# A four-stage graph network on one core: the combined node pass stores 136-column rows whole, and the attention scalars from a compact buffer

## The chip, the core and the metric

One core of a Trainium2 chip runs the whole network in one launch. The metric is the device time of that launch in microseconds (us). Engines are named as in the profile: PE multiplies matrices, DVE, ACT and POOL work element by element, SP only issues transfers, and 16 DMA engines move the data. POOL also issues the gathers and scatters by index.

## What is computed

There are 50,000 nodes with 128 features and 25,000 edges, sorted by destination. Four graph layers follow each other, each added to its input and normalised over the features:

```python
x = _layernorm(x + L0(x, src, dst, edge_weight, ...))
x = _layernorm(x + L1(x, ...))            # five rounds of propagation
x = _layernorm(x + L2(x, edge_attr_128, src, dst, ...))
x = _layernorm(x + L3(x, edge_index, ...))

# L3, attention with 4 heads of 32 columns:
xt = (x @ W.T + bias).reshape(n, H, C)
alpha_src = jnp.sum(xt * a_src, axis=-1)
alpha_dst = jnp.sum(xt * a_dst, axis=-1)
alpha = leaky_relu(alpha_src[row] + alpha_dst[col], 0.2)
# softmax of alpha over the edges of one destination, then
out = segment_sum(xt[row] * alpha[..., None], col)
```

So L3 needs, for each node, 128 columns of xt and 4 scalars as a source (136 columns with the 4 scalars as a destination).

## The kernel before

The kernel is a sequence of stages, each a block in which every engine runs a program of its own and waits on semaphores. Edge stages go over 200 tiles of 125 edges. Node stages go over the 50,000 rows in 30 chunks (`chunk`, lines 682 to 686): partition p owns 390 consecutive rows, and a chunk is 13 of them per partition, so that a chunk's rows of one partition are consecutive in DRAM. The last 80 rows are a chunk of their own. Node buffers are cut out of the tile `big` by `areas`, three slots each.

The change is in the combined node pass (lines 1850 to 2143). It finishes L2 and begins L3 for each chunk c:

- SP (`load`, `store`): waits until x3 of chunk c is ready, stores it (L1904), issues the two loads for chunk c+3 (x2n, L1898, and agg, L1899), waits until the transformed rows of chunk c are ready, and stores them: `xt_d`, 132 columns (L1908), and `ad_d`, 4 columns (L1909). All five go through one queue. Both stores read the same buffer O3, whose rows are 136 columns wide, so neither reads consecutive memory: a partition's data are 13 pieces of 528 bytes, and 13 pieces of 16 bytes.
- POOL: scales for the normalisation of chunk c (`ln_scale`, L743, L744, L746, L749), then the sums of chunk c+2 (L1930, L1933, and after a wait for its two loads L1937, L1941).
- DVE: for chunk c+1 `rows` (L2001, statistics L1989, L2011), which wait for POOL and PE, then for chunk c `transformed`: bias added from PSUM into O3 (L2019), and a 1x1 memset (L2025) that only carries the signal `d_o` to SP.
- ACT: copies of transposes out of PSUM for chunk c+1 (L2036), between them the normalisation of chunk c (L2042), which waits for L749, then the copies L2053.
- PE: transposes and products of chunk c+1 (L2106, L2116), then of chunk c (L2127, L2137).

The next stage (lines 2146 to 2192) gathers, for each of the 200 tiles of edges, the 132-column rows of `xt_d` by source into G (L2162) and the 4 columns of `ad_d` by destination into AD (L2165), both issued by POOL in turn; ACT copies the rows into `xts` (L2192), DVE adds the scalars (L2180).

Of the kernel before, what the change touches and what calls it, by code (L numbers as in the profile page):

```python
# [7 lines left out]
P, D = 128, 128  # L8
N, E = 50000, 25000
TE = 125  # L10
T = E // TE
GR = 4
U = 2 * GR
# [9 lines left out]
HEADS, CH = 4, D // 4  # L23
# [3 lines left out]
NJ = 13  # L27
CHUNKS = NC_ // NJ
SLOTS = 3
# [6 lines left out]
def build(nc, x0, src, dst, ea, ew, w0, b0, w1, b1, gamma, beta, w2, b2, we, be, coef, linw, linb, asrc, adst, out):  # L36
# [3 lines left out]
    def sb(name, shape, dt=F32):  # L40
        return ctx.enter_context(nc.sbuf_tensor(name, shape, dt))
# [3 lines left out]
    def sem(name):  # L45

        phase.append(nc.alloc_semaphore(name=name))
        return phase[-1]
# [16 lines left out]
    def dram(name, shape, dt=F32):  # L65
        return nc.dram_tensor(name, shape, dt).ap()

    with ctx:
# [7 lines left out]
        x1 = dram("x1", (N, D))  # L76
        x2n = dram("x2n", (N, D + 1))
        x3 = dram("x3", (N, D))
        xt_d = dram("xt_d", (N, D + HEADS))
        ad_d = dram("ad_d", (N, HEADS))  # L80
        lastpos = dram("lastpos", (N, 1), I32)
        pair_d = dram("pair_d", (T * P, 2))
# [32 lines left out]
        G = sb("G", [P, RG, D + HEADS])  # L115
# [19 lines left out]
        col = sb("col", [P, 8])  # L135
# [546 lines left out]
        def chunk(t, c, w):  # L682

            if c is None:
                return t[TAIL0:N, 0:w].unsqueeze(1)
            return t[0:TAIL0, :].rearrange("(p n) f -> p n f", n=NC_)[:, bass.ds(c * NJ, NJ), 0:w]
# [15 lines left out]
        def areas(widths, at=0, slots=2):  # L702

            got = []
            for w in widths:
                got.append([big[:, at + s * NJ * w:at + (s + 1) * NJ * w].rearrange("p (n f) -> p n f", f=w)
                            for s in range(slots)])
                at += slots * NJ * w
            return got
# [311 lines left out]
        flatY, flatG = Y[:].rearrange("p s f -> p (s f)"), G[:].rearrange("p s f -> p (s f)")  # L1021
# [9 lines left out]
        at = TG * P + TG * T // 2  # L1031
# [617 lines left out]
        at = U * CW  # L1649
# [198 lines left out]


        DX = D + 2 * HEADS  # L1850
        X2L, YL, X3, O3 = areas([D + 1, D, D, DX], slots=SLOTS)
        at = SLOTS * NJ * (3 * D + 1 + DX)
        W2 = big[:, at:at + D]
        B2 = big[:, at + D:at + 2 * D]
        LW = big[:, at + 2 * D:at + 5 * D].rearrange("p (b i) -> p b i", b=3)
# [28 lines left out]
        with nc.Block() as block:  # L1884
            @block.sync
            def _(sp):
                with nc.allow_non_contiguous_dma(reason="short columns"):
                    sp.dma_start(W2, w2).then_inc(d_w, 16)
                    sp.dma_start(B2, b2.partition_broadcast(P)).then_inc(d_w, 16)
                    sp.dma_start(LW, linw.rearrange("b o i -> o b i")).then_inc(d_w, 16)  # L1890
                    sp.dma_start(CF, coef.partition_broadcast(P)).then_inc(d_w, 16)
                    sp.dma_start(AC[:, 0, :], asrc.rearrange("b q h c -> (q h c) b")).then_inc(d_w, 16)
                    sp.dma_start(AC[:, 1, :], adst.rearrange("b q h c -> (q h c) b")).then_inc(d_w, 16)
                    sp.dma_start(AC[:, 2, :], linb.rearrange("b o -> o b")).then_inc(d_w, 16)
                def load(c, s, n):
                    np_, nj = size(c)
                    sp.wait_ge(d_t, before_chunk(c, QA))
                    sp.dma_start(X2L[s][0:np_, 0:nj, :], chunk(x2n, c, D + 1)).then_inc(d_ld[s], 16)  # L1898
                    sp.dma_start(YL[s][0:np_, 0:nj, :], chunk(agg, c, D)).then_inc(d_ld[s], 16)  # L1899

                def store(c, s, n, later):
                    np_, nj = size(c)
                    sp.wait_ge(d_x3[s], n + 1)
                    sp.dma_start(chunk(x3, c, D), X3[s][0:np_, 0:nj, :]).then_inc(d_sx[s], 16)  # L1904
                    if later:
                        load(*later)
                    sp.wait_ge(d_o[s], n + 1)
                    sp.dma_start(chunk(xt_d, c, D + HEADS), O3[s][0:np_, 0:nj, 0:D + HEADS]).then_inc(d_so[s], 16)  # L1908
                    sp.dma_start(chunk(ad_d, c, HEADS), O3[s][0:np_, 0:nj, D + HEADS:DX]).then_inc(d_so[s], 16)  # L1909
                turns = CHUNKS // SLOTS  # L1910
                for u in range(SLOTS):
                    load(u, u, 0)
                with sp.Fori(0, turns - 1) as i:
                    for u in range(SLOTS):
                        store(SLOTS * i + u, u, i, (SLOTS * i + SLOTS + u, u, i + 1))
                for u in range(SLOTS):
                    store(CHUNKS - SLOTS + u, u, turns - 1, (None, 0, turns) if u == 0 else None)
                store(None, 0, turns, None)
                for s in range(SLOTS):
                    sp.wait_ge(d_sx[s], 16 * (turns + (1 if s == 0 else 0)))  # L1920
                    sp.wait_ge(d_so[s], 32 * (turns + (1 if s == 0 else 0)))
# [38 lines left out]
            def _(dve):  # L1960
# [53 lines left out]
                def transformed(c, s, n):  # L2014
                    np_, nj = size(c)
                    dve.wait_ge(d_so[s], 32 * n)
                    for q, js in groups(c, 3):
                        dve.wait_ge(d_q, before_chunk(c, QB) + q + 1)
                        ins = nc.vector.tensor_tensor(  # L2019
                            O3[s][0:np_, js[0]:js[-1] + 1, :],  # L2020
                            bank(6 + q % 2, 3 * DX).rearrange("p (j f) -> p j f", f=DX)[0:np_, 0:len(js), :],
                            B3X[0:np_, :].unsqueeze(1).to_broadcast([np_, len(js), DX]), ALU.add)
                        ins.then_inc(d_oc, 1)
                    dve.wait_ge(d_oc, before_chunk(c, QB) + len(groups(c, 3)))
                    nc.vector.memset(col[0:1, 7:8], 0.0).then_inc(d_o[s], 1)  # L2025
                one_ahead(dve, rows, transformed)

            @block.scalar
# [117 lines left out]
        XW = D + HEADS  # L2146
        xts = big[:, 0:T * XW].rearrange("p (t f) -> p t f", f=XW)
        AL = cf[:, 0:T * HEADS].rearrange("p (t h) -> p t h", h=HEADS)
        AD = sb("AD", [P, U, HEADS])
        e_idx, e_cp = sem("e_idx"), sem("e_cp")  # L2150
        e_got, e_gad = pool_sems("e_got", U), pool_sems("e_gad", U)
        with nc.Block() as block:
            @block.gpsimd
            def _(pool):
                with pool.Fori(0, IT) as i:
                    for j in range(U):
                        steady(pool, 2 * i + j // GR + 1)
                        if j % GR == 0:

                            pool.wait_ge(e_idx, 2 * i + j // GR + 1)  # L2160
                            pool.wait_ge(e_cp, 2 * i + j // GR + 1)
                        pool.indirect_dma_start(G[:, j, 0:XW], None, xt_d, bass.IndirectOffsetOnAxis(  # L2162
                            ap=ridx[:, j:j + 1], axis=0)).then_inc(e_got[j], 16)
                        steady(pool)
                        pool.indirect_dma_start(AD[:, j, :], None, ad_d, bass.IndirectOffsetOnAxis(  # L2165
                            ap=sidx[:, j:j + 1], axis=0)).then_inc(e_gad[j], 16)

            @block.vector
            def _(dve):
                nc.vector.tensor_copy(ridx[:], src_i[:, 0:U])  # L2170
                nc.vector.tensor_copy(sidx[:], dst_i[:, 0:U]).then_inc(e_idx, 2)
                credit(e_cp, 2)
                with dve.Fori(0, IT) as i:
                    for h in range(2):
                        js = slice(GR * h, GR * h + GR)
                        steady(dve, 16 * i + 16)
                        for q in range(GR * h, GR * h + GR):
                            dve.wait_ge(e_got[q], 16 * i + 16)
                            dve.wait_ge(e_gad[q], 16 * i + 16)
                        nc.vector.tensor_tensor(AL[:, bass.ds(U * i + GR * h, GR), :], G[:, js, D:XW], AD[:, js, :],  # L2180
                                                ALU.add)
                        nc.vector.tensor_copy(ridx[:, js], src_i[:, bass.ds(U * i + U + GR * h, GR)])
                        nc.vector.tensor_copy(sidx[:, js], dst_i[:, bass.ds(U * i + U + GR * h, GR)]).then_inc(e_idx, 1)

            @block.scalar
            def _(act):
                with act.Fori(0, IT) as i:
                    for h in range(2):
                        steady(act, 16 * i + 16)
                        for q in range(GR * h, GR * h + GR):  # L2190
                            act.wait_ge(e_got[q], 16 * i + 16)
                        nc.scalar.copy(xts[:, bass.ds(U * i + GR * h, GR), :], G[:, GR * h:GR * h + GR, :]).then_inc(e_cp, 1)  # L2192

# [231 lines left out]
```

## Time and profile before

| | |
|---|---|
| median of 3 timed runs | 9566.44 us (9566.18 to 9572.16) |
| the profiled execution's own time | 9559.96 us |
| its span in the trace | 9558.2 us |
| POOL busy | 6656.3 us, 70% |
| PE busy | 5802.3 us, 61% |
| DVE busy | 4949.1 us, 52% |
| combined node pass in the trace | about 7928 to 8500 us |
| gather stage of L3 | about 8500 to 9000 us |

How to read it: busy shares over the whole span mix stages with different limits. In a row of the timeline the columns are the start, the duration, the engine, the line and operation, the tiles, the count, and in brackets the idle time before it with what ended it. A row of SP shows how long SP was held by issuing a transfer, not the transfer itself.

### The profile page before, as it was taken

To read this page: it belongs to the slowest core of one execution; us is meant where nothing else is said; L and a number is where in the kernel's file an instruction comes from. 1 tells how busy PE (TensorE), PEld (TensorE's weight loads), DVE (VectorE), ACT (ScalarE), POOL (GpSimd) and SP (SyncE) were. 2 spreads that over 40 slices of the span, in tenths; PEclk is the share of its full clock that TensorE was granted. 3 is DMA by queue.
4 is the path that set the end of the run, shared out by engine and by line. 5 is a ranking of instruction groups with operands and counts; after the bars stand their busy time and mean duration, and the time that the engine had idled before them with its cause. 6 is when DMAs were issued, how large, how long until landed. Compare 5 with 4: busy or idle time off the path is not lost. (4 is left out here: it accounts for less than half of the span.)

```text
span 9558.2 us, 109668 instructions
## 1 busy us (share of the span) xinstructions
PE 5802.3 (61%) x24229; PEld 4310.9 (45%) x24229; DVE 4949.1 (52%) x12073; ACT 2449.6 (26%) x6228; POOL 6656.3 (70%) x6509
## 2 busy tenths in 40 slices
PE   4646557767775777765776756677651775630190
PEld 2436224555554555544555544555540665630170
DVE  5668765553335743345733346533357774520277
ACT  0115000222224222233222233222246113420006
POOL 4767663577777777777777777777766777767566
PEclk8765776775555855556855557755555887865555
DMA  3127101567755756655668656778656227961017
GB/s 145 43 94 257 25 2 31 115 116 101 101 100 103 135 105 100 102 100 111 126 105 99 102 99 125 116 100 100 101 106 228 64 68 156 193 107 28 20 31 327
DMA packets 564302, 1024.19 MB, mean 107 GB/s; under 512 B 192219, under 2 KB 275724, under 8 KB 563556
## 3 DMA queue, kind: packets, MB, share of 16 engines
q0 software_dynamic: 192032, 330.29, 31.3%
q1 hardware_dynamic: 354372, 588.76, 20.0%
q10 hardware_dynamic: 17664, 102.61, 2.6%
q14 instruction: 159, 1.30, 0.1%
q8 instruction: 75, 1.23, 0.1%
HBM read 561.87 MB, written 471.67 MB: 108 GB/s over the span
## 5 line engine op out<-in xcount | busy, mean ns | idle before, releaser
L1018 POOL DMA_INDIRECT G<-tab,gidx x4000 | 3952.7, 988 | 1622.0 <-issue 1407.3
L1365 PE MATMUL PS<-M,G 128*128 128x128 f32 x6400 | 2226.2, 472 | 1344.2 <-DMA G<-tab,gidx 949.2
L1365 PEld LDWEIGHTS PS<-M,G 128*128 128x128 f32 x6400 | 1539.3, 310 | 2052.8 <-DMA G<-tab,gidx 1463.8
L1313 ACT ACTIVATE M<-ident,wz 128x128 f32<-128x128 f32 x3200 | 1021.4, 390 | 2382.4 <-DVE UO L1421 1238.9
L1421 DVE TENSOR_TENSOR_SCAN UO<-keyrow,UT,PS 128x512 f32<-128x512 f32 (+1 forms) x400 | 512.0, 1280 | 1296.5 <-PE PS L1365 1296.5
L1421 DVE TENSOR_TENSOR_SCAN UT<-keyrow,UO,PS 128x512 f32<-128x512 f32 (+1 forms) x400 | 512.0, 1280 | 1193.1 <-PE PS L1365 1193.1
L758 ACT ACTIVATE big<-big,nb,rs 128x128 f32<-128x128 f32 x1173 | 461.3, 480 | 426.3 <-POOL nb L749 358.7
L1443 DVE TENSOR_TENSOR Y<-PS,big 128x512 f32<-128x512 f32 x800 | 536.3, 670 | 14.6 <-PE PS L1386 7.5
L1105 POOL DMA_INDIRECT Y<-pair_d,G x400 | 402.6, 1007 | 201.5 <-issue 130.6
L1390 PE MATMUL PS<-ident,UT 128*128 128x128 f32 x1600 | 419.2, 417 | 9.6 <-DVE UT L1421 9.6
L1390 PE MATMUL PS<-ident,UO 128*128 128x128 f32 x1600 | 420.6, 418 | 0.0
L1368 PE MATMUL PS<-ident,G 128*128 128x128 f32 x800 | 192.1, 310 | 348.8 <-DMA G<-tab,gidx 298.6
L1331 ACT ACTIVATE M<-PS,tcol,scol 128x512 f32<-128x512 f32 x200 | 155.4, 777 | 834.5 <-PE PS L1368 834.5
L1257 PE MATMUL PS<-big 128*128 128x400 f32 x800 | 321.2, 527 | 44.6 <-DVE G L1151 27.4
L1390 PEld LDWEIGHTS PS<-ident,UT 128*128 128x128 f32 x1600 | 340.3, 227 | 15.6 <-DVE UT L1421 15.6
L1390 PEld LDWEIGHTS PS<-ident,UO 128*128 128x128 f32 x1600 | 345.0, 228 | 0.0
L2269 PE MATMUL PS<-ident,cf 128*100 128x128 f32 x8 | 2.0, 424 | 526.5 <-DVE cf L2215 526.5
L450 POOL DMA_INDIRECT G<-in_x,ridx x200 | 206.7, 1033 | 157.4 <-DVE ridx L520 95.2
L2313 POOL DMA_INDIRECT agg<-Y,sidx x200 | 197.3, 987 | 153.7 <-DVE Y L2364 105.3
L902 POOL DMA_INDIRECT gidx<-lastpos,src_i x200 | 229.9, 1150 | 103.1 <-issue 68.4
L1368 PEld LDWEIGHTS PS<-ident,G 128*128 128x128 f32 x800 | 110.1, 149 | 411.4 <-DMA G<-tab,gidx 359.8
L1384 PE MATMUL PS<-cf 128*128 128x512 f32 x400 | 260.9, 741 | 8.3 <-DVE UT L1421 4.2
(500 smaller groups left out, 11257.3 us busy)
## 6 DMA issues: line engine op xcount, KB each, us to landing
tab<-Y SPq DMA_DIRECT2D x1050, 256.0 KB, 2.9
big<-agg SPq DMA_DIRECT2D x90, 832.0 KB, 11.4
G<-tab,gidx POOLq DMA_INDIRECT x4000, 4.0
WR<-w_d SPq DMA_DIRECT2D x200, 256.0 KB
big<-x SPq DMA_DIRECT2D x60, 832.0 KB, 4.9
xt_d<-big SPq DMA_DIRECT2D x30, 858.0 KB
x2n<-big ACTq DMA_DIRECT2D x30, 838.5 KB, 3.5
big<-x2n SPq DMA_DIRECT2D x30, 838.5 KB, 11.9
```

The lines of the kernel that those rows point to most:

```text
L758: ins = nc.scalar.activation(X[0:np_, j, 0:D], V[0:np_, j, :], ACT.Identity, scale=rs[0:np_, s, j:j + 1], bias=nb[0:np_, s, j:j + 1])
L902: pool.indirect_dma_start(gidx[:, t:t + 1], None, lastpos, bass.IndirectOffsetOnAxis(ap=src_i[:, t:t + 1], axis=0)).then_inc(g_got, 16)
L1018: pool.indirect_dma_start(G[:, t % RG, 0:D], None, tab_in(k), bass.IndirectOffsetOnAxis(ap=gidx[:, t:t + 1], axis=0)).then_inc(l_got[t % R ...
L1105: pool.indirect_dma_start(GS[:, t, :], None, pair_d, bass.IndirectOffsetOnAxis(ap=G2[:, t:t + 1], axis=0)).then_inc(o_got, 16)
L1257: ins = nc.tensor.matmul(bank2(n % 2)[:, j, :], OH[:, 2 * n + j, :], CT, start=True, stop=True)
L1313: ins = nc.scalar.activation(M[:, GR * h + j, :], ident[:], ACT.Copy, scale=wz[:, bass.ds((NB * i + q) * GR + j, 1)])
L1365: ins = nc.tensor.matmul(PS[:, FT_[h], j, :], G[:, s, 0:D], M[:, GR * h + j, :], start=True, stop=True)
L1368: ins = nc.tensor.transpose(PS[:, FT_[h], j, :], G[:, s, 0:D], ident[:])
L1384: nc.tensor.matmul(bank(BK_[h]), QR[:, q % NG, :], BD, start=True, stop=False)
L1390: ins = nc.tensor.transpose(PS[:, BK_[h], j, :], UR[h][:, j, :], ident[:])
L1421: nc.vector.tensor_tensor_scan(S[h], keyrow[:, bass.ds(tile * P, GR * P)], half if k == 0 else bank(FT_[h]), S[1 - h][:, GR * P - 1:GR * P ...
L1443: nc.vector.tensor_tensor(group_of(Y, q % NG), PS[:, BK_[h], :, :], zt_at((NB * i + q) * GR).rearrange("p (s f) -> p s f", f=D), ALU.add). ...
```

## The change

Rows of `xt_d` become 136 columns wide, and the store takes the whole buffer O3, whose pieces of one partition then join into one run of 7072 bytes. The destination's scalars are copied by DVE (in place of the memset that carried the signal) into a compact buffer AO of 4 columns, and stored from it: one run of 208 bytes per partition. The gather takes 136 columns per row, into a view GX of the same tile G, and its readers are pointed at GX. The diff:

```diff
-        xt_d = dram("xt_d", (N, D + HEADS))
+        xt_d = dram("xt_d", (N, D + 2 * HEADS))
...
-        X2L, YL, X3, O3 = areas([D + 1, D, D, DX], slots=SLOTS)
-        at = SLOTS * NJ * (3 * D + 1 + DX)
+        X2L, YL, X3, O3, AO = areas([D + 1, D, D, DX, HEADS], slots=SLOTS)
+        at = SLOTS * NJ * (3 * D + 1 + DX + HEADS)
...
-                    sp.dma_start(chunk(xt_d, c, D + HEADS), O3[s][0:np_, 0:nj, 0:D + HEADS]).then_inc(d_so[s], 16)
-                    sp.dma_start(chunk(ad_d, c, HEADS), O3[s][0:np_, 0:nj, D + HEADS:DX]).then_inc(d_so[s], 16)
+                    sp.dma_start(chunk(xt_d, c, DX), O3[s][0:np_, 0:nj, :]).then_inc(d_so[s], 16)
+                    sp.dma_start(chunk(ad_d, c, HEADS), AO[s][0:np_, 0:nj, :]).then_inc(d_so[s], 16)
...
-                    nc.vector.memset(col[0:1, 7:8], 0.0).then_inc(d_o[s], 1)
+                    nc.vector.tensor_copy(AO[s][0:np_, 0:nj, :], O3[s][0:np_, 0:nj, D + HEADS:DX]).then_inc(d_o[s], 1)
...
+        GX = flatG[:, 0:U * DX].rearrange("p (s f) -> p s f", f=DX)
...
-                        pool.indirect_dma_start(G[:, j, 0:XW], None, xt_d, bass.IndirectOffsetOnAxis(
+                        pool.indirect_dma_start(GX[:, j, :], None, xt_d, bass.IndirectOffsetOnAxis(
...
-                        nc.vector.tensor_tensor(AL[:, bass.ds(U * i + GR * h, GR), :], G[:, js, D:XW], AD[:, js, :],
+                        nc.vector.tensor_tensor(AL[:, bass.ds(U * i + GR * h, GR), :], GX[:, js, D:XW], AD[:, js, :],
...
-                        nc.scalar.copy(xts[:, bass.ds(U * i + GR * h, GR), :], G[:, GR * h:GR * h + GR, :]).then_inc(e_cp, 1)
+                        nc.scalar.copy(xts[:, bass.ds(U * i + GR * h, GR), :], GX[:, GR * h:GR * h + GR, 0:XW]).then_inc(e_cp, 1)
```

No instruction changes its place in any engine's program, and the number of instructions stays.

## Rows read from the trace of the kernel before

**Rows 1.** Busy time by stretch: us, each engine's busy us, clock, DMA share, GB/s.
```profile
8200.00:8300.00 100.00, 66.50 (x425) 59.04 (x425) 51.14 (x236) 45.51 (x112) 73.49 (x45) 0.86 1.02 180
```
**Rows 2.** Transfers in the stretch 8000 to 8400 us, packets by size, main queue.
```profile
DMA packets 85696, 76.70 MB, mean 192 GB/s; under 512 B 39958, under 2 KB 77247, under 8 KB 85695
...
q1 hardware_dynamic: 85695, 76.68, 102.9%
```
**Rows 3.** Timeline of SP's issues: start, us held, line, tiles.
```profile
7972.06 0.36 SPq L1904 DMA_DIRECT2D x<-big  x1
...
7973.23 1.06 SPq L1899 DMA_DIRECT2D big<-agg  x1
7979.74 0.41 SPq L1908 DMA_DIRECT2D xt_d<-big  x1
...
7986.45 0.34 SPq L1904 DMA_DIRECT2D x<-big  x1
...
8016.76 3.31 SPq L1904 DMA_DIRECT2D x<-big  x1
...
8430.70 2.14 SPq L1904 DMA_DIRECT2D x<-big  x1
...
8485.05 1.82 SPq L1909 DMA_DIRECT2D ad_d<-big  x1
8486.91 2.21 SPq L1904 DMA_DIRECT2D x<-big  x1
```
**Rows 4.** Timeline of POOL: start, us, line, idle before.
```profile
7965.27 0.21 POOL L749 TENSOR_TENSOR nb<-nb,rs 128x13 f32<-128x13 f32 x1
...
7979.64 0.22 POOL L749 TENSOR_TENSOR nb<-nb,rs 128x13 f32<-128x13 f32 x1
...
7993.65 0.22 POOL L749 TENSOR_TENSOR nb<-nb,rs 128x13 f32<-128x13 f32 x1
...
7999.40 3.40 POOL L1937 TENSOR_TENSOR big<-big 128x1664 f32<-128x1664 f32 x1 [2.25 <-DMA big<-agg]
...
8456.86 0.22 POOL L749 TENSOR_TENSOR nb<-nb,rs 128x13 f32<-128x13 f32 x1
```
**Rows 5.** Who waited for the load of agg (L1899): us, times.
```profile
  POOL big L1937: 100.3, 27
```
**Rows 6.** Transfers in the stretch 9400 to 9450 us (last node pass).
```profile
DMA packets 3586, 21.29 MB, mean 426 GB/s; under 512 B 388, under 2 KB 388, under 8 KB 3586
```
**Rows 7.** Transfers in 7980 to 7984 us, the first xt_d store.
```profile
DMA packets 1577, 0.83 MB, mean 208 GB/s; under 512 B 0, under 2 KB 1577, under 8 KB 1577
```
**Rows 8.** Issue of agg in 7971 to 7979 us: KB, us to landing.
```profile
big<-agg SPq DMA_DIRECT2D x1, 832.0 KB, 7.0
```
**Rows 9.** Timeline of ACT, the first copy of a turn.
```profile
7979.53 0.58 ACT L2036 COPY HT<-PS 128x512 f32<-128x512 f32 x1 [1.30 <-PE PS L2106]
...
7992.99 0.58 ACT L2036 COPY HT<-PS 128x512 f32<-128x512 f32 x1 [1.30 <-PE PS L2106]
```
**Rows 10.** Timeline of DVE around the signal d_o.
```profile
7992.97 0.06 DVE L2025 MEMSET col<- 1x1 f32 x1
7994.94 1.13 DVE L2001 SCALAR_TENSOR_TENSOR big<-PS,rin,big 128x128 f32<-128x128 f32 x4 [1.91 <-PE PS L2116]
```
**Rows 11.** Groups by line, a DVE copy of 132 elements.
```profile
L407 DVE COPY G<-carry 1x132 f32<-1x132 f32 x50 | 10.6, 212 | 0.8 <-PE PS L2381 0.8
```
**Rows 12.** Timeline of POOL in the last node pass, a short instruction twice.
```profile
9483.88 1.99 POOL L743 TENSOR_SCALAR rs<-mv 128x13 f32<-128x13 f32 x1 [0.61 <-DVE mv L735]
...
9489.62 0.26 POOL L743 TENSOR_SCALAR rs<-mv 128x13 f32<-128x13 f32 x1 [0.62 <-DVE mv L735]
```
**Rows 13.** Timeline of DVE in the last node pass, at the same moment.
```profile
9483.85 1.89 DVE L2399 TENSOR_TENSOR big<-big 128x1664 f32<-128x1664 f32 x1
```
**Rows 14.** Groups by line on POOL, the two gathers of the next stage.
```profile
L2162 POOL DMA_INDIRECT G<-xt_d,ridx x200 | 188.8, 944 | 87.4 <-issue 60.6 <-DVE note L170 26.8
L2165 POOL DMA_INDIRECT AD<-ad_d,sidx x200 | 188.8, 944 | 61.0 <-issue 51.5 <-ACT big L2192 9.5
```

## The prediction

> **What bounds the kernel now.** I read the busy times by stage first, since the change sits in one stage of some 570 us in a span of 9558.2 us. In the combined node pass no engine is near full: in 100 us PE is busy 66.50, DVE 51.14, ACT 45.51 and POOL 73.49, while the DMA engines stand at a share of 1.02 and move only 180 GB/s [rows 1]. The view of the transfers says why: of 85,696 packets in 400 us, 39,958 are under 512 bytes and another 37,289 under 2 KB, and the queue's packets took 102.9% of 16 engines' time [rows 2]. A full chunk stores 13 x 128 = 1664 pieces of 16 bytes and 1664 of 528 bytes; its x3 store and its two loads are only 128 long pieces each. The last node pass, whose transfers are all of that long kind, moves 426 GB/s [rows 6]. So the DMA engines are the bound here through the number of pieces, not through bytes.
>
> SP's timeline gives the pace. The x3 stores of chunks 3 and 26 start at 8016.76 and 8430.70 [rows 3]: 23 periods in 413.94 us, 18.0 us each. POOL's timeline shows where that reaches the engines: L1937 waits for the load of agg, 27 times and 100.3 us in all [rows 5], first at 7999.40 [rows 4].
>
> The same timeline also shows the pace without that wait, and this is what I use most. L749, which ends POOL's scaling of a chunk, starts at 7965.27, 7979.64 and 7993.65 [rows 4]. In these first periods the stores had not piled up yet, POOL ran nearly without a gap, and the period was 14.37 and then 14.01 us. The second one is POOL's own instructions end to end.
>
> **The change, part by part.**
>
> *Transfers of a chunk.* At 426 GB/s [rows 6] the three long transfers (832 + 838.5 + 832 KB, 2.56 MB) take 6.0 us. The first xt_d store went at 208 GB/s averaged over 7980 to 7984 [rows 7], but it was issued at 7979.74 [rows 3] and did not fill that stretch: 0.88 MB in some 3 to 4 us; I take 3. That leaves 18.0 - 6.0 - 3.0 = 9.0 us for the 1664 pieces of 16 bytes, so the smallest store is the dearest. After the change the xt_d store is 0.905 MB in 128 long pieces, 2.1 us, and ad_d is 128 pieces instead of 1664: 9.0 / 13 = 0.7 us if a piece keeps its price. Sum: 6.0 + 2.1 + 0.7 = 8.8 us a chunk, well under 14.01. The DMA engines stop being the bound.
>
> The Trainium skill (DMA: Bandwidth & Descriptors, Specifications) puts full rate at 512 bytes and more, with a read-modify-write below. By that rule the 528-byte store was at full rate already (2.1 us, and 9.9 for the small one) and making it whole wins nothing; the trace speaks against the rule for this store [rows 6, 7]. The sum would be the same by either, since both stores change together.
>
> *What is late next.* With the DMA free, POOL needs the load of chunk c+3 some 10.7 us after the x3 store of chunk c is issued: issue at 7986.45, and POOL was ready for L1937 at 7999.40 - 2.25 = 7997.15 [rows 3, 4]. In the one case with no strided store ahead, the x3 store went out at 7972.06 and agg was issued at 7973.23 [rows 3] and landed 7.0 us later [rows 8]: 8.2 us. So the load comes 2.5 us before it is needed, and POOL's wait (100.3 us) goes away. The other circle, ACT to PE to DVE and back, needs 7992.99 - 7979.53 = 13.46 us [rows 9], 0.55 less than POOL. POOL becomes the bound, at 14.01 us.
>
> From chunk 0 to chunk 28 L749 went from 7965.27 to 8456.86 [rows 4]: 491.59 us for 28 periods. After: 14.37 + 27 x 14.01 = 392.64 us. **Gain 98.95 us.** The last two chunks do not wait for loads, and I leave them.
>
> *The copy in place of the memset.* It moves 52 elements per partition. The nearest row is a copy of 132 elements in 212 ns [rows 11]; the memset took 60 ns [rows 10]. I take 0.2 us. On DVE itself it is covered: after the memset DVE idles 1.91 us for PE [rows 10]. But it may hold up POOL. In the last node pass a POOL instruction that began 0.03 us after a DVE addition of two SBUF tiles took 1.99 us, as long as that addition (1.89) [rows 12, 13], against 0.26 for the same instruction with no such neighbour [rows 12]. POOL is now the bound, so a copy that shuts it out costs its own time: 28 x 0.2 = 5.6 us. Bounds: 0, if it falls in a gap of POOL, and 5.9 (28 x 0.212). A gain is excluded, as the memset was already hidden. I take **5.6 us lost**, because POOL now has hardly a gap.
>
> [...]
>
> *The end of the pass.* The last x3 store's issue held SP 2.21 us, and the ad_d issue ahead of it 1.82 [rows 3]; free ones take 0.36 [rows 3] and about 0.4. That is 1.85 + 1.4 = 3.25 us; the two last copies take 0.3 back. **Gain 2.9 us.** Between nothing and 3.25.
>
> *The gather stage.* POOL issues a gather of 528-byte rows in 944 ns and one of 16-byte rows in 944 ns too [rows 14]: the length of a row does not matter to the issue, and the issues set the pace of that stage. 544 instead of 528 bytes: nothing. The ACT copy keeps its size and its cover; POOL waited for it 9.5 us in all [rows 14]. If a longer landing doubled that, 9.5 us would be lost: the bound on that side.
>
> *Sum.* -98.95 + 5.6 - 2.9 = -96.3 us. Against the profiled execution's 9559.96 this gives 9463.7; that execution lies 6.5 us below the median 9566.44, and timed runs are what is compared, so I carry the difference over: 9566.4 - 96.3 = **9470 us**, 1.0% faster. (About 0.2%, 19 us, is what a measurement of this kernel can tell from no change.)
>
> **The rivals.**
>
> *DVE waits for POOL at the copy, and the circle through DVE becomes the bound.* In the uncovered period the memset came at 7992.97, 0.7 us before POOL's L749 [rows 4, 10]. A copy there would wait for the POOL instruction under way, about 0.6 us, inside the 1.91 us of slack. If the phases slip so that it meets POOL's L1933 (3 us), L2001 starts about a microsecond late and the period grows to some 15.0 us. Gain 28 x (17.56 - 15.0) + 2.9 = 74.6: **9492 us**. For it: the lock seen in [rows 12, 13]. Against it: the 1.91 us.
>
> *The small store keeps its price* (its cost is not in the number of pieces, or its 13 pieces of a partition do not join, so that the change does not do what it says). Then a chunk needs 6.0 + 2.1 + 9.0 = 17.1 us of DMA instead of 18.0, the copy is hidden under POOL's waits, and some 25 periods win 0.9 us: 22 us, **9544 us**. Against it: the x3 store and the loads are of the same form, 13 rows side by side on both ends, and they do go as 128 pieces (8,448 packets over 2 KB in 22 chunks is 384 each) [rows 2].
>
> *Slower: a gather of longer rows costs POOL more to issue.* If a 544-byte row had to be cut in two and the issue of 944 ns doubled, the 200 gathers of L2162 would take 189 us more, and the sum would be +93: **9659 us**. It decides from 96.3 / 200 = 0.48 us per gather. Against it: 528-byte and 16-byte rows cost the same [rows 14], though one is 33 times as long.
>
> **How the numbers follow.** The forecast gets 0.76, the copy that waits 0.10, the small store that keeps its price 0.12, the dearer gather 0.02. Range: the fast end is the sum without the copy's cost and with the whole end gain, 9566 - 102 = 9464, less some 8 us for the spread between single executions and for a faster PE clock in the last chunks: 9456. The slow end takes in the first rival and loads that come a microsecond late in 14 or so periods: 9506. Faster by over 0.2%: 0.76 + 0.10 + two thirds of 0.12 = 0.94; within 0.2%: 0.04; slower: 0.02.
>
> **What would show it.** In the pass, packets under 512 bytes nearly vanish and the DMA share falls to some 0.6 (8.8 of 14.2 us); SP's ad_d issues drop to about 0.4 us; L1937 has no wait for DMA; x3 stores follow each other every 14.0 to 14.3 us; a POOL instruction beside the copy is longer by up to 0.2 us; the gathers keep 944 ns. I am wrong if POOL still waits for loads, if it waits for DVE's statistics (L2011) in every chunk, or if the copy takes over a microsecond.

## The result and the profile after

The changed kernel takes **9449.06 us** (median of 4 runs, 9439.55 to 9455.72) against 9566.51 us before: ratio 0.9881, 95% interval 0.9868 to 0.9893, a gain of 117.5 us. The forecast was 9470 us with a range down to 9456. The direction and the new bound came as forecast; the gain was larger than the range allowed. One of the 11 executions of place_only, a kernel of the experiments, took 15,695.65 us, far from the other ten, and is left out of its ratio.

The transfers of the pass in the profile after, 300 us out of its middle (columns as in [rows 1] and [rows 2]):

```profile
8012.89:8312.89 300.00, 231.86 (x1657) 196.91 (x1655) 206.41 (x959) 191.70 (x476) 286.44 (x170) 0.98 0.64 246
```
```profile
DMA packets 15349, 73.90 MB, mean 246 GB/s; under 512 B 4529, under 2 KB 4529, under 8 KB 15349
...
q1 hardware_dynamic: 15349, 73.90, 63.7%
```

POOL is busy for 286.44 of 300 us, where it was 73.49 of 100 [rows 1]. The granted clock of TensorE is 0.98 here and was 0.86 there, but a chunk's time is now POOL's own, so it is not the clock that sets the pace. The DMA share fell from over 1 to 0.637, and the packets of 300 us from some 64,000 to 15,349 [rows 2]. POOL has no wait for a DMA left; the largest of its waits from 8000 to 8350 us is for itself (us in all, times, longest):

```profile
POOL big L1941 <- POOL big L1937: 4.2, 25, 0.2
```

The timeline of POOL, chunks 0, 1 and 28 and the first gather of the next stage:

```profile
7968.88 0.21 POOL L749 TENSOR_TENSOR nb<-nb,rs 128x13 f32<-128x13 f32 x1
...
7983.25 0.21 POOL L749 TENSOR_TENSOR nb<-nb,rs 128x13 f32<-128x13 f32 x1
...
8362.89 0.22 POOL L749 TENSOR_TENSOR nb<-nb,rs 128x13 f32<-128x13 f32 x1
...
8396.12 1.12 POOL L2163 DMA_INDIRECT G<-xt_d,ridx  x1 [16.93 <-DVE note L170]
```

From chunk 0 to chunk 28 it is 394.01 us, against 491.59 [rows 4]: 97.6 us gained. From there to the first gather it is 33.23 us; before, the first gather came at 8500.85, 43.99 us after [rows 4]: 10.8 us gained. SP's issues, one full chunk in the middle and the last ones of the pass:

```profile
8313.48 0.33 SPq L1904 DMA_DIRECT2D x<-big  x1
8314.11 0.35 SPq L1898 DMA_DIRECT2D big<-x2n  x1
8314.65 1.06 SPq L1899 DMA_DIRECT2D big<-agg  x1
8320.36 0.35 SPq L1908 DMA_DIRECT2D xt_d<-big  x1
8320.89 0.36 SPq L1909 DMA_DIRECT2D ad_d<-big  x1
8327.55 0.33 SPq L1904 DMA_DIRECT2D x<-big  x1
...
8391.94 0.44 SPq L1909 DMA_DIRECT2D ad_d<-big  x1
```

In the middle of the pass no issue holds SP any more (compare the 3.31 and 2.14 us in [rows 3]). The last store is issued at 8391.94 + 0.44 = 8392.38, and DVE begins the next stage at 8394.94, 2.6 us later. Before, DVE's next stage began 9.6 us after the last issue (below). The gathers kept their price, where [rows 14] had 944 ns:

```profile
L2163 POOL DMA_INDIRECT G<-xt_d,ridx x200 | 188.9, 945 | 77.6 <-issue 60.6 <-DVE note L170 16.9
```

### The profile page after: what moved, and what is told of

Same layout as the page of the kernel before. It is cut to its first block and busy times, and to the rows that moved or that the text cites. A ratio compares the mean times of both kernels' runs of the same rounds, so it can differ in the third digit from the quotient of the medians.

```text
span 9453.9 us, 109668 instructions
## 1 busy us (share of the span) xinstructions
PE 5807.2 (61%) x24229; PEld 4281.7 (45%) x24229; DVE 4952.6 (52%) x12073; ACT 2449.6 (26%) x6228; POOL 6665.9 (71%) x6509
## 3 DMA queue, kind: packets, MB, share of 16 engines
q1 hardware_dynamic: 262212, 589.56, 17.4%
## 5 line engine op out<-in xcount | busy, mean ns | idle before, releaser
L1365 PE MATMUL PS<-M,G 128*128 128x128 f32 x6400 | 2257.8, 476 | 1299.6 <-DMA G<-tab,gidx 902.2
L1384 PE MATMUL PS<-cf 128*128 128x512 f32 x400 | 261.0, 741 | 14.6 <-DVE UT L1421 7.6
```

Of the source, the lines that this page charges most:

```text
L1365: ins = nc.tensor.matmul(PS[:, FT_[h], j, :], G[:, s, 0:D], M[:, GR * h + j, :], start=True, stop=True)
L1384: nc.tensor.matmul(bank(BK_[h]), QR[:, q % NG, :], BD, start=True, stop=False)
```

## The experiments

All runs were timed beside the kernel before on the same chip. The chips differ (A is the one of the result; it is not on record whether it is one of the others): the kernel before took 9566.5 us on A, 9697.7 on B, 9533.4 and later 9535.7 on C, and 9569.3 on D. So times are compared within a chip, and stretches of the profile between chips. Even ratios compare only roughly between chips: kernels whose pass is the same within 1 us have 0.987 to 0.988 on A, B and D and 0.990 on C. In the tables "0 to 28" is the time from POOL's L749 of chunk 0 to that of chunk 28, "end" from there to the first gather, "period" the mean of the chunks 6 to 26, and "DMA" the share of the main queue in 300 us of the pass times the period: the DMA work of a chunk in us. (In some kernels an added line shifts the line numbers; L749 is then L750.)

| kernel | chip | ratio to before, 95% | 0 to 28 | end | period | DMA |
|---|---|---|---|---|---|---|
| before | A | 1 | 491.6 | 44.0 | 17.9 | 1.03 of 17.9 |
| changed | A | 0.9881 (0.9868 to 0.9893) | 394.0 | 33.2 | 14.06 | 8.95 |
| again | B | 0.9875 (0.9861 to 0.9890) | 393.4 | 33.1 | 14.04 | 9.00 |
| ad_only | B | 0.9868 (0.9854 to 0.9882) | 393.4 | 37.3 | 14.04 | 10.9 |
| rows_only | B | 0.9952 (0.9939 to 0.9965) | 479.7 | 39.6 | 17.6 | 17.4 |
| copy5 | B | 0.9870 (0.9856 to 0.9885) | 393.2 | 34.8 | 14.03 | |
| before_again | C | 0.9997 (0.9988 to 1.0006) | 485.6 | 42.7 | 17.6 | |
| place_only | C | 1.0002 (0.9993 to 1.0011) | 470.5 | 41.9 | 17.0 | |
| no_copy | C | 0.9905 (0.9889 to 0.9920) | 393.8 | 33.9 | 14.05 | |
| pool_relief | C | 0.9891 (0.9876 to 0.9906) | 379.2 | 33.6 | 13.53 | |
| before_b | D | 1.0000 (0.9990 to 1.0009) | 505.4 | 43.5 | 18.4 | |
| rows_only_b | D | 0.9931 (0.9914 to 0.9948) | 445.9 | 41.7 | 16.1 | 15.9 |
| extra128 | D | 0.9882 (0.9866 to 0.9899) | 393.8 | 37.6 | 14.06 | 12.1 |
| extra60 | D | 0.9882 (0.9865 to 0.9898) | 394.0 | 39.1 | 14.07 | 11.4 |
| extra16 | C | 0.9899 (0.9882 to 0.9915) | 393.7 | 35.8 | 14.04 | 10.1 |
| extra4pad | C | 0.9904 (0.9887 to 0.9920) | 393.8 | 37.1 | 14.06 | 9.95 |
| extra4 | C | 0.9955 (0.9938 to 0.9972) | 435.9 | 42.8 | 15.8 | 15.3 |

**The changed kernel again** (no edit).

> The changed kernel once more, to tell its own spread from the gain. The profile showed the combined pass shorter by 97.6 us up to the scaling of chunk 28 and by 10.8 us from there to the first gather, 108.4 us together. Theory A (the whole gain is made in this pass, the rest is spread between executions): median ratio 0.988 to 0.989 again, 9450 to 9460 us, executions spread over some 15 us. Theory B (something outside the pass got faster too): the median stays below 9450 us, a gain of over 117 us, and some stage before 7928 us is shorter in the new profile by about 10 us.

The median moved with the chip (9575.5 beside 9697.7), so the microseconds of both theories missed. The ratio is 0.9875, just below theory A's 0.988 to 0.989 but with them in its interval; the gain of 122 us is one that theory B allowed. The stretches in the pass repeat to 0.6 us, and this run alone can't say where the rest was made.

**Only the compact buffer.** Against the kernel before:

```diff
-        X2L, YL, X3, O3 = areas([D + 1, D, D, DX], slots=SLOTS)
-        at = SLOTS * NJ * (3 * D + 1 + DX)
+        X2L, YL, X3, O3, AO = areas([D + 1, D, D, DX, HEADS], slots=SLOTS)
+        at = SLOTS * NJ * (3 * D + 1 + DX + HEADS)
...
-                    sp.dma_start(chunk(ad_d, c, HEADS), O3[s][0:np_, 0:nj, D + HEADS:DX]).then_inc(d_so[s], 16)
+                    sp.dma_start(chunk(ad_d, c, HEADS), AO[s][0:np_, 0:nj, :]).then_inc(d_so[s], 16)
...
-                    nc.vector.memset(col[0:1, 7:8], 0.0).then_inc(d_o[s], 1)
+                    nc.vector.tensor_copy(AO[s][0:np_, 0:nj, :], O3[s][0:np_, 0:nj, D + HEADS:DX]).then_inc(d_o[s], 1)
```

> Only the compact buffer for the 4 scalars; rows stay 132 columns wide, stored in 528-byte pieces. Theory A (the 16-byte pieces cost 9.0 us of DMA a chunk, the 528-byte pieces 3.0): DMA per chunk 6.0 + 3.0 + 0.7 = 9.7 us, still under POOL's 14.01, so the pass is as short as with the whole change: 9450 us, within 5 us of the changed kernel; the end of the pass (last scaling of a full chunk but one, to the first gather) about 33 us as in the changed kernel. Rival (the 528-byte pieces carry half of the price or more): 6.0 + 6.0 + 6.0 or so before, now 12.7 us plus the wait for a late load, period 15 us or more, 9480 us.

The pass is as short as with the whole change, 393.4 us, with the 528-byte pieces still there. The queue's share in 300 us:

```profile
DMA packets 49039, 73.67 MB, mean 246 GB/s; under 512 B 4529, under 2 KB 40972, under 8 KB 49039
...
q1 hardware_dynamic: 49039, 73.67, 77.6%
```

0.776 x 14.04 = 10.9 us of DMA work, 1.9 us more than the whole change and far under 14. So the compact buffer alone gives the whole gain up to chunk 28, and the whole rows, once it is there, shorten only the end, from 37.3 to 33.1 us on this chip. (The forecast for ad_only had an end of 33 and 9.7 us of DMA work: both missed.) The timed runs can't tell the 4 us: again has 9575.5 us and ad_only 9568.0, with overlapping intervals.

**Only the whole rows**, twice. Against the changed kernel:

```diff
-                    sp.dma_start(chunk(ad_d, c, HEADS), AO[s][0:np_, 0:nj, :]).then_inc(d_so[s], 16)
+                    sp.dma_start(chunk(ad_d, c, HEADS), O3[s][0:np_, 0:nj, D + HEADS:DX]).then_inc(d_so[s], 16)
...
-                    nc.vector.tensor_copy(AO[s][0:np_, 0:nj, :], O3[s][0:np_, 0:nj, D + HEADS:DX]).then_inc(d_o[s], 1)
+                    nc.vector.memset(col[0:1, 7:8], 0.0).then_inc(d_o[s], 1)
```

> Only the whole rows of 136 columns; the 4 scalars stored from the wide buffer in 1664 pieces of 16 bytes, no copy on DVE. Theory A (16-byte pieces are the price): DMA per chunk 6.0 + 2.1 + 9.0 = 17.1 us, period 17.1 instead of 18.0, gain some 22 us: 9544 us; the end of the pass stays at about 44 us. Rival (the 528-byte pieces carry half or more): period 14 to 15 us, gain 75 us or more, 9490 us or less. If the end's 10.8 us belongs to the 528-byte pieces, the end falls to about 33 us here.

> Whole rows with the 16-byte pieces kept, on the same chip as before_b. The first run gave 479.7 us from chunk 0 to 28 and a DMA share of 0.99 at a period of 17.6 us. Theory A (the 16-byte pieces hold the pace, the 528-byte ones cost little on top of them): 5 to 20 us less than before_b in the pass and 3 to 5 us less at its end. Rival (the 41 us that the timed runs showed are made in the pass): 35 us or more less than before_b.

> The kernel before once more, beside rows_only_b on one chip. Its combined pass took 491.6 us (chunk 0 to 28) in the first profile, 485.6 in the second, 470.5 in the kernel with only the placement changed, so the pass that waits for DMA scatters while the changed one (393.2 to 394.0 in four profiles) does not. Theory A (the price of the small pieces differs between executions and chips): a further value between 470 and 510 us here, and the landing of the last stores 8 to 10 us after their issue. Theory B (the first profiles are typical and the rest lies before the pass): 486 to 492 us.

The 16-byte pieces alone keep the DMA engines full (rows_only, then rows_only_b):

```profile
q1 hardware_dynamic: 38375, 59.57, 98.6%
```
```profile
q1 hardware_dynamic: 40926, 64.85, 99.1%
```

But their price is no constant. The first run needed 17.4 us a chunk, close to the 17.1 forecast, the second 15.9. Beside before_b (505.4 us) rows_only_b gained 59.5 us up to chunk 28, which fits its rival and not the 5 to 20 us of its theory A. The kernel before itself has 491.6, 485.6 and 505.4 us in three profiles and 470.5 with a change of placement that did nothing to the time. before_b keeps within its theory A. How much whole rows win while the small pieces are there differs as much. In the profiles it is 12 us (two chips) and 59 us (one chip); timed beside the kernel before it is 41 us on B (9656.3 against 9697.7) and 64 us on D (9505.3 against 9569.3). At the end of the pass rows_only_b gained 1.8 us, not the 3 to 5 forecast. The timed 41 us lie between the 22 us of the first run's theory A and the 75 us of its rival, so neither held, and its end fell to 39.6 us where about 44 was forecast.

**Four more copies** on DVE per chunk, into spare buffers (AX4, taken by `areas` like AO):

```diff
+                    for again in AX4:
+                        nc.vector.tensor_copy(again[s][0:np_, 0:nj, :], O3[s][0:np_, 0:nj, D + HEADS:DX])
                     nc.vector.tensor_copy(AO[s][0:np_, 0:nj, :], O3[s][0:np_, 0:nj, D + HEADS:DX]).then_inc(d_o[s], 1)
```

> The changed kernel with four more copies of the same shape per chunk on DVE, into spare buffers. The copy takes 0.207 us. Theory A (a copy within SBUF shuts POOL out for its duration or waits for the POOL instruction under way): POOL's 14.01 us grow by up to 4 x 0.2 = 0.8 us a chunk, 28 x 0.8 = 22 us, or the copies take far more than 0.207 us each where POOL is busy. Rival (no lock between this copy and POOL; the cost of the one copy is nothing): five copies end 0.83 us later, inside DVE's idle 1.8 to 2.0 us for PE, the period stays 14.07 us and the time within 3 us of the changed kernel.

The rival holds: 393.2 us, no slower than one copy, and 9570.4 us beside again's 9575.5. The timelines of DVE and of POOL at one chunk:

```profile
8310.34 0.55 DVE L2026 COPY big<-big 128x52 f32<-128x52 f32 x4
8310.81 0.20 DVE L2027 COPY big<-big 128x52 f32<-128x52 f32 x1
8312.33 1.13 DVE L2001 SCALAR_TENSOR_TENSOR big<-PS,rin,big 128x128 f32<-128x128 f32 x4 [1.32 <-PE PS L2118]
```
```profile
8308.50 2.46 POOL L746 TENSOR_TENSOR rs<-rs,minus_half 128x13 f32<-128x13 f32 x1
8311.03 0.22 POOL L749 TENSOR_TENSOR nb<-nb,rs 128x13 f32<-128x13 f32 x1
```

Four copies run inside POOL's L746 (8308.50 to 8310.96), which takes its usual 2.46 us, and take no longer themselves. L746 is a long instruction on 13 elements, so a short lock could hide in it. The first chunk shows the other order: the four copies begin at 8086.42 and last 0.55 us, and two short POOL instructions begin among them.

```profile
8086.57 0.22 POOL L749 TENSOR_TENSOR nb<-nb,rs 128x13 f32<-128x13 f32 x1
8086.73 0.19 POOL L1930 COPY big<-nsrc 128x13 f32 x1
```

They take their usual 0.22 and 0.2 us. Neither engine waits for the other here.

**The memset back, no copy.** The buffer is cleared once, so this kernel leaves the destination's term out of the attention:

```diff
+                for s_ in range(SLOTS):
+                    nc.vector.memset(AO[s_], 0.0)
...
-                    nc.vector.tensor_copy(AO[s][0:np_, 0:nj, :], O3[s][0:np_, 0:nj, D + HEADS:DX]).then_inc(d_o[s], 1)
+                    nc.vector.memset(col[0:1, 7:8], 0.0).then_inc(d_o[s], 1)
```

> The changed kernel with the memset in place of the copy again and the compact buffer cleared once, so the 4 destination scalars are stored as zeros: it leaves the destination's term out of the attention. Five copies cost nothing in the pass (393.2 us from chunk 0 to 28, as with one). So theory A: 393 to 394 us again and the same time as the changed kernel within 3 us. Rival (the first copy has a price that further ones share): 388 us or less.

393.8 us: the copy costs nothing in the pass. (The changed kernel was not timed on this chip. extra16 and extra4pad, which keep the copy, have 0.9899 and 0.9904 there against 0.9905.)

**The kernel before with a profile of its own, and the placement alone** (xt_d's DRAM made as large as in the changed kernel, rows still 132 wide).

> The kernel before, with a profile of its own on this chip. Three of the four kernels sent so far gained 6 to 25 us more than their profiles show in and after the combined pass (again: 122 us against some 109; only the compact scalars: 130 against 105; only whole rows: 41 against 16). Theory A (spread, since the two profiles lie in different executions): ratio 1.000, and the first scaling of the combined pass starts within the 8072 to 8096 us of the others. Theory B (stages before the pass are slower in this kernel): it starts at 8100 us or later in this profile, although their code is the same, and the combined pass itself is 491 us from chunk 0 to 28 with 44 us behind it, as on the first chip.

> The kernel before, except that xt_d takes as much DRAM as in the changed kernel (its rows stay 132 columns, stored and gathered as before), so that the tensors allocated behind it, the tables of L1 among them, lie where they lie in the changed kernel. Theory A (placement does nothing): ratio 1.000 within 0.001. Theory B (placement moves the L1 stages): 9 us or more faster than before, all of it before the combined pass.

Neither found anything outside the pass: ratios 0.9997 and 1.0002, the first L749 at 7957.05 and 7956.24 us, against 7961.63 in no_copy, and 1057 to 1058 us from the first gather to the end in all three. (The 8072 to 8100 us of the forecast were those of chip B.) What they did show is the scatter of the pass itself: their profiled executions differ by 17.5 us, and 15.1 of these lie between chunk 0 and 28.

**POOL relieved.** L1933 reduced to one row of 13; the kernel leaves out b2 x (in-degree + 1) for the others:

```diff
-                    nc.gpsimd.tensor_tensor(b, wide(B2, np_, nj), R1[0:np_, 0:nj].unsqueeze(2)
-                                            .to_broadcast([np_, nj, D]), ALU.mult).then_inc(d_r1b, 1)
+                    nc.gpsimd.tensor_tensor(BT[0:np_, 0:1, :], wide(B2, np_, 1), R1[0:np_, 0:1].unsqueeze(2)
+                                            .to_broadcast([np_, 1, D]), ALU.mult).then_inc(d_r1b, 1)
...
+                nc.vector.memset(BT, 0.0)
```

> The changed kernel with the bias product of POOL (L1933, 3.0 us a chunk) reduced to one of 13 rows: it leaves out the term b2 x (in-degree + 1) for the other rows. Theory A (POOL's instructions, 14.01 us a chunk end to end, are the new bound and the circle of ACT, PE and DVE, 13.46 us, is next): period 13.4 to 13.5 us, 28 x 0.6 = 17 us faster than the changed kernel. Rival (the circle contains POOL's scaling, so relief elsewhere on POOL moves nothing, or DMA is next at 14): the period stays at 14.0 us.

The period falls to 13.53 us and 0 to 28 to 379.2, 14.6 us less than no_copy on the same chip. Timed, the medians differ by 17.6 us (9428.4 against 9446.0). POOL now waits for the circle (who waited for whom, 350 us):

```profile
POOL rs L743 <- DVE mv L2012: 43.0, 26, 8.3
```

So POOL was the bound of the changed kernel and the circle of ACT, PE and DVE is next, half a microsecond below (L2012 is L2011 here).

**The price of short pieces by itself.** Five kernels: the changed kernel with one more store a chunk of 1664 pieces out of O3 into a scratch tensor. For 60 columns:

```diff
+        scr_d = dram("scr_d", (N, 60))
...
                     sp.dma_start(chunk(ad_d, c, HEADS), AO[s][0:np_, 0:nj, :]).then_inc(d_so[s], 16)
+                    sp.dma_start(chunk(scr_d, c, 60), O3[s][0:np_, 0:nj, DX - 60:DX]).then_inc(d_so[s], 16)
...
-                    dve.wait_ge(d_so[s], 32 * n)
+                    dve.wait_ge(d_so[s], 48 * n)
```

The others have 128, 16 and 4 columns; extra4pad writes 4 columns into rows of 136.

> The changed kernel with one more store per chunk: 1664 pieces of 512 bytes, read out of the wide buffer, into a scratch tensor. The changed kernel's DMA work is 0.637 x 14.05 = 8.9 us a chunk. Theory A (pieces of 512 bytes cost about what those of 528 do, 3 to 4 us for 1664): DMA share 0.85 to 0.92, period 14.05 us, no change in time beyond 5 us. Rival (price per piece, whatever its length): 8.9 + 8.5 = 17.4 us a chunk, 85 us slower than the changed kernel.

> The same with 1664 pieces of 240 bytes. The Trainium skill (DMA: Bandwidth & Descriptors, Specifications) puts a read-modify-write below 512 bytes. Theory A (pieces below 512 bytes pay alike, whatever their length): about the 8.5 us of the 16-byte store, period some 17.4 us, 90 us slower than the changed kernel. Rival (price by bytes or by piece, with no step at 512): no dearer than the 512-byte pieces, period 14.05 us, no change in time.

> The changed kernel with one more store per chunk: 1664 pieces of 16 bytes into a scratch tensor of 4 columns, so that 13 of them lie side by side in DRAM, as the ad_d store of the kernel before. Pieces of 240 bytes added 2.4 us of DMA a chunk and those of 512 bytes 3.1. Theory A (16-byte pieces have a price of their own): DMA share 0.97 or more, period 16.5 us or more, 70 us or more slower than the changed kernel, and the executions scatter. Rival (the price of the old ad_d store came from something else, as the wide buffer being read by two stores): at most 2.4 us added, period 14.05 us.

> The same 1664 pieces of 16 bytes, but each into a DRAM row of its own of 544 bytes, so that no two pieces are neighbours. Theory N (neighbours: pieces that lie side by side in DRAM hold each other up): 2 to 3 us added, period 14.05 us, as fast as the changed kernel. Theory L (length: a 16-byte write is dear by itself): as slow as the pieces side by side, period 16.5 us or more.

> The same with 1664 pieces of 64 bytes side by side. Theory N or L with a step between 16 and 64 bytes: some 2 us added, period 14.05 us. If pieces of 64 bytes are as dear as those of 16, period 16.5 us or more, and the step lies between 64 and 240 bytes.

The main queue in 300 us of extra128, extra60, extra16, extra4pad and extra4:

```profile
q1 hardware_dynamic: 52108, 92.58, 85.9%
```
```profile
q1 hardware_dynamic: 52310, 82.69, 80.8%
```
```profile
q1 hardware_dynamic: 52327, 76.37, 71.8%
```
```profile
q1 hardware_dynamic: 52313, 74.51, 70.8%
```
```profile
q1 hardware_dynamic: 45685, 67.41, 97.1%
```

Times the period, less the 8.95 us of the changed kernel: 512-byte pieces add 3.1 us a chunk, 240-byte 2.4, 64-byte 1.1, 16-byte pieces apart 1.0, and **16-byte pieces side by side 6.3**. Only the last leaves the 14.05 us of POOL (period 15.8) and costs time: on one chip its median is 9494.0 against 9444.2 for the same pieces apart. extra128 fits its theory A; in extra60 theory A is refuted and the rival holds. Theory N holds, with sizes that were off: it is not the length alone, nor the number. But extra4 cost less than both its theory A and theory L asked (period 15.8, not 16.5; 50 us, not 70), and its executions do not scatter (9489.9 to 9497.4 us). 16-byte writes next to each other in DRAM cost what the same writes apart, or 64-byte ones next to each other, do not. By which mechanism isn't shown, nor whether it is their being next to each other or the small stretch of DRAM that they share: rows of their own spread them over 34 times as much.

## Why the prediction was wrong, and where it was right

*What bounds the pass, and what is late next: right.* DMA work of 8.8 us a chunk was forecast, 8.95 measured; POOL at 14.01 forecast, 14.06 measured; POOL's wait for loads gone. The first circle with POOL out of the way was 13.46 in the forecast and 13.53 in pool_relief.

*The term of the copy: mis-sized, by the whole 5.6 us.* The step was "so a copy that shuts it out costs its own time: 28 x 0.2 = 5.6 us". The copy took 0.207 us but shut nobody out: with the memset the stretch is the same (393.8). From chunk 0 to 28 the profile has 394.01 where 392.64 was forecast without the copy, so the forecast of the 28 periods was 1.4 us too low, and 4.2 us of the 5.6 are left in the sum. The analogy with [rows 12, 13] failed: there DVE reads two SBUF tiles, here one, and the POOL instruction is another. Which of the two matters was not tested. The first rival falls with it. The Trainium skill (SBUF — State Buffer, Who interferes with whom) has a DVE instruction with one SBUF input keep off POOL outside the 2-port modes, and a copy in such a mode lock it out; no run here shows in which mode this copy was.

*The end of the pass: the step that failed most, by 7.9 us.* The step was "The last x3 store's issue held SP 2.21 us, and the ad_d issue ahead of it 1.82": it counted only SP's held issues, a gain of 2.9 us with an upper bound of 3.25, and put the landing of the last stores at nothing. From L749 of chunk 28 to the end of the last issue 33.20 us became 29.49, a gain of 3.7. The other 7.0 us lie behind that issue. The SP and DVE timelines of the kernel before show the gap, and between them the DMA engines (columns as in [rows 1]):

```profile
8489.64 0.42 SPq L1909 DMA_DIRECT2D ad_d<-big  x1
```
```profile
8490.00:8492.00 2.00, 0.00 (x0) 0.00 (x0) 0.00 (x0) 0.00 (x0) 0.00 (x0) 0.50 0.41 31
8492.00:8494.00 2.00, 0.00 (x0) 0.00 (x0) 0.00 (x0) 0.00 (x0) 0.00 (x0) 0.50 0.00 0
...
8496.00:8498.00 2.00, 0.00 (x0) 0.00 (x0) 0.00 (x0) 0.00 (x0) 0.00 (x0) 0.50 0.00 0
```
```profile
8499.67 0.17 DVE L2170 COPY ridx<-src_i 128x8 int32<-128x8 int32 x1 [14.08 <-PEq L52]
```

That is 9.6 us from the end of the last issue to the next stage, against 2.6 after; SP's program ends with a wait for the landing of every store. For the last 7.6 us of it the trace has no packet on any DMA engine: no queue is being worked off, and what is late is the report that the data have landed. From the last issue to the next stage it is 8.5 us in rows_only and 4.9 in ad_only, so the 16-byte pieces lengthen it most; it is 8.7 in extra4 and 4.5 in extra4pad, so here too it matters how they lie. Why the report is late isn't shown.

*Together* 96.3 + 4.2 + 7.9 = 108.4 us, the gain of the two profiles from chunk 0 of the pass to the first gather.

*The rest, 9 us, is the choice of single executions.* The two profiled ones differ by 9559.96 - 9455.72 = 104.2 us, since chunk 0 came 3.6 us later in the changed kernel's (7968.88 against 7965.27). Before's lay 6.6 us below its median and the changed kernel's 6.7 above: 117.5. I carried the first difference over and allowed too little for the second. More than that, I read the price of the pass from one execution: 0 to 28 was 491.6 us in it, and is 485.6 to 505.4 in others. The changed pass doesn't scatter (393.4 to 394.0), so the gain does, with the kernel before. On chip C the kernel with the memset back gained 87 us and one that even carries an extra store 91.5 (extra4pad), on B the changed kernel gained 122. The range of 9456 to 9506, a gain of 60 to 110 us, had no term for this, and whether a gain falls within it is luck of the chip: those on C do. Where the scatter of the small pieces comes from stays open.

*The split of the DMA work: half right.* "9.0 us for the 1664 pieces of 16 bytes": rows_only shows 17.4 - 8.95 + 0.7 = 9.1 us (0.7 being the forecast's estimate for the compact store), rows_only_b 7.7, extra4 6.3. "3 us" for the 528-byte store was low: 4.0, the 1.9 measured on top of the forecast's 2.1 for whole rows. But the price "if a piece keeps its price" was a wrong reading that happened to do no harm: the cost is in how the short pieces lie, not in their number: 1664 of them apart cost 1.0 us.

*The other rivals.* The small store did not keep its price, and the gathers did keep theirs (945 ns). But the second rival's own price was wrong: with the small store as it was, whole rows gained 41 and 64 us timed, not 22.

## What to carry to other kernels

A store whose pieces are a few bytes long and lie side by side in DRAM is worth a small copy into a compact buffer, however few its bytes: here 26 KB a chunk held up 3.4 MB. Joining longer strided pieces brings little once another engine is the bound (1.9 us of DMA work a chunk and 4 us at the end here). Where a stage is bound by such transfers, read its price from several executions, and count the landing of its last stores into its end.

## What the runs showed of the hardware that was not expected

1664 stores of 16 bytes side by side added 6.3 us of DMA work a chunk, the same stores 544 bytes apart 1.0, and 64-byte ones side by side 1.1. The price of one piece has no step between 240 and 512 bytes: 2.4 and 3.1 us for 1664 pieces. The Trainium skill (DMA: Bandwidth & Descriptors, Specifications) gives 512 bytes as the least for full rate, with a read-modify-write below. Here 512-byte pieces moved 0.85 MB in 3.1 us, some 275 GB/s, against 387 for the changed kernel's own transfers (73.90 MB in 0.637 x 300 us), so 512 bytes were not enough; and those of 240 bytes were slower by the byte (166 GB/s) but not dearer by the piece. With short pieces in the queue a landing was reported up to 7.6 us after the DMA engines had gone idle. And DVE copies of 52 elements within SBUF ran beside POOL instructions that read SBUF with neither slowed (0.55 us for four copies, 2.46 and 0.22 us for POOL's).
